# Edge attention on one NeuronCore: TensorE's weighted sums of batch b-2 stand in front of the transposes of batch b instead of behind them

## The reference, cut to what matters

```python
Q = (h @ Wq.T + bq).reshape(-1, H, DH)
K = (h @ Wk.T + bk).reshape(-1, H, DH)
V = (h @ Wv.T + bv).reshape(-1, H, DH)
scores = jnp.einsum('ehd,egd->ehg', Q[src], K[tgt]) / jnp.sqrt(jnp.float32(DH))
attn = jax.nn.softmax(scores, axis=-1)
msg = jnp.einsum('ehg,egd->ehd', attn, V[tgt]).reshape(-1, HID)
msg = msg + Ee[et]
proj = msg @ Wo.T + bo
return jax.ops.segment_sum(proj, src, num_segments=n_nodes)
```

## Time and profile before

| What | us |
|---|---|
| median of 3 runs | 7294.34 (7294.27 to 7296.85) |
| the profiled execution's own time | 7286.34 |
| its span, first to last instruction | 7284.5 |
| VectorE busy in the span | 5184.5 (71%) |
| GpSimd busy | 4463.2 (61%) |
| TensorE busy, products | 4321.9 (59%) |
| mean granted clock of TensorE | 0.823 of full speed |

### The profile page before, as it was taken

The page is one execution under the profiler, slowest core; times in us unless marked ns, Lnnn a source line. Parts: engine busy times, 40 slices in busy tenths (PEclk is TensorE's granted clock), DMA queues, the critical chain, the costliest instruction groups (busy, mean ns, idle before and its releaser), DMA issues. The chain is left out here.

```text
span 7284.5 us, 179506 instructions
## 1 busy us (share of the span) xinstructions
PE 4321.9 (59%) x60555; PEld 3475.4 (48%) x60555; DVE 5184.5 (71%) x12108; ACT 1183.6 (16%) x2828; POOL 4463.2 (61%) x3974
## 2 busy tenths in 40 slices
PE   0000388885245546788877788876888885355541
PEld 0000266663134435677765677764777764133331
DVE  6999877777445565677765677755777755688877
ACT  0000022220011111122210222210222211122210
POOL 5888777777177730777751777741777740577720
PEclk9999999995555558999998999998999997555555
DMA  0000000001144433666613666614676510344420
GB/s 30 1 4 1 2 1 1 1 1 27 30 123 131 131 85 110 182 201 193 185 34 118 188 198 192 175 31 125 191 201 193 165 27 10 98 111 111 110 63 18
DMA packets 708570, 691.60 MB, mean 95 GB/s; under 512 B 234981, under 2 KB 589355, under 8 KB 708165
## 3 DMA queue, kind: packets, MB, share of 16 engines
q0 software_dynamic: 227328, 446.06, 22.5%
q1 hardware_dynamic: 480846, 240.51, 11.9%
HBM read 766.03 MB, written 77.58 MB: 116 GB/s over the span
## 5 line engine op out<-in xcount | busy, mean ns | idle before, releaser
L1669 POOL DMA_INDIRECT kvring<-kvtab,oth x1776 | 1973.5, 1111 | 822.5 <-issue 420.4
L1069 POOL DMA_INDIRECT e_hg<-htab,oth_d x992 | 1014.9, 1023 | 817.4 <-issue 763.5
L1720 PE MATMUL ea_pss<-ea_qb,ea_kT 128*128 128x128 f32 x7104 | 1020.5, 277 | 0.0
L1720 PEld LDWEIGHTS ea_pss<-ea_qb,ea_kT 128*128 128x128 f32 x7104 | 946.3, 194 | 16.3
L1764 ACT ACTIVATE ea_kT<-ea_pst 128x512 f32<-128x512 f32 x888 | 482.0, 594 | 2013.4 <-PE ea_pst L1708 1984.2
L1708 PE MATMUL ea_pst<-ident,kvring 128*128 128x128 f32 x3552 | 488.2, 281 | 464.7 <-DMA kvring<-kvtab,oth 464.3
L241 POOL DMA_INDIRECT steps<-or_rec,or_rplacei x392 | 567.5, 1448 | 135.0 <-issue 135.0
L1708 PEld LDWEIGHTS ea_pst<-ident,kvring 128*128 128x128 f32 x3552 | 385.5, 142 | 543.0 <-DMA kvring<-kvtab,oth 332.3
L1804 DVE TENSOR_REDUCE ea_sc<-ea_pss 128x64 f32<-128x1024 f32 x444 | 540.8, 1218 | 53.1 <-PE ea_pss L1720 53.0
L1832 DVE TENSOR_TENSOR ea_mix<-ea_hot,ea_att 128x1024 f32<-128x1024 f32 (+1 forms) x444 | 544.9, 1227 | 0.2
L1731 PE MATMUL ea_psg<-ea_mix,kvring 128*64 128x64 f32 x14208 | 518.1, 227 | 12.8 <-DVE ea_mix L1832 12.8
(11 more groups left out here) (506 smaller groups left out, 8332.7 us busy)
## 6 DMA issues: line engine op xcount, KB each, us to landing
ea_qb<-qtab SPq DMA_DIRECT2D x1776, 64.0 KB
qtab<-at_qst SPq DMA_DIRECT2D x75, 512.0 KB, 3.3
kvring<-kvtab,oth POOLq DMA_INDIRECT x1776
e_stack<-ohtab SPq DMA_DIRECT2D x744, 32.0 KB
kvtab<-at_kvst SPq DMA_DIRECT2D x75, 256.0 KB, 2.7
e_hg<-htab,oth_d POOLq DMA_INDIRECT x992
ea_mk<-mtab SPq DMA_DIRECT2D x444, 3.0 KB
htab<-Hd SPq DMA_DIRECT2D x2, 3200.0 KB, 11.6
```

The lines of the kernel that those rows point to most:

```text
L1069: pool.indirect_dma_start(out=hg[:, b % RING, u, :], out_offset=None, in_=htab, in_offset=bass.IndirectOffsetOnAxis(ap=oth[:, b * 4 + u:b ...
L1669: pool.indirect_dma_start(out=kv[:, b % R, u, :], out_offset=None, in_=kvtab, in_offset=bass.IndirectOffsetOnAxis(ap=oth[:, b * QB + u:b * ...
L1720: mm = pe.matmul(ps_s[r % 2][:, u, k * 2 * HN:(k + 1) * 2 * HN], kT[:, r % 2, u, k, :], qb[:, r, u, :], start=False, stop=True, skip_group ...
```

## The change

In the two places of TensorE's list where `turn` and `gather` are called together, the call of `gather(b - 2)` moves in front of `turn(b)`. Nothing is added or removed, and the lists of the other four engines are the same, row for row.

```diff
                 for r in range(1, R):
-                    turn(r, 0, r, True)
                     if r >= 2:
                         gather(r - 2, 0, r - 2, False)
+                    turn(r, 0, r, True)
                     score(r, 0, r, r >= 2)
                 with pe.Fori(1, NQ // R) as i:
                     for r in range(R):
                         b = i * R + r
-                        turn(b, i, r, True)
                         if r >= 2:
                             gather(b - 2, i, r - 2, True)
                         else:
                             gather(b - 2, i - 1, r + 2, True)
+                        turn(b, i, r, True)
                         score(b, i, r, True)
```

## The result

The changed kernel takes 7564.57 us (median of 4 runs, 7561.62 to 7567.53), the kernel before 7295.6 us in the same comparison (7294.27 to 7303.79, 4 runs). The ratio is 1.036, with a 95% interval of 1.034 to 1.038. The profiled execution took 7562.66 us, with a span of 7560.9, against 7286.34 before.

The account below looks back on a forecast made before the run. GpSimd's gather pace was taken as the bound, 5.60 us a batch; a new closed loop of 6.22 us adds 266.5 us, layer starts 12 and the profile-to-median gap 8, giving 7573 us, range 7470 to 7640.

Parts of the forecast that it names:

- The bound of before: GpSimd's gather issues, one per 1.41 us and four a batch, set the old period of about 5.6 us.
- The closed loop: Transposes, spread, exponential, weights, sums, then transposes again: 6.22 us a batch, +266.5 us over 432 periods.
- The last term: On TensorE, from the first sum to the first transpose: 1.12 us, kept between 1.00 and 1.25.
- the leg: From the start of the transposes to the end of the weights, over ScalarE and VectorE: 5.00 us.
- Nothing gained behind the transposes: On TensorE, the sums were hidden behind ScalarE's spread, so scores still start 2.27 us after the transposes.
- The starts of the layers: Batches 2 and 3 of each layer now wait for the weights: 4.0 us a layer, 12 us in all.
- The wait for rows: TensorE's 464.3 us wait for gathered rows ahead of the transposes goes, with 4.7 us to spare.
- The rival by which it falls: TensorE's clock falls to 1.2 GHz: 9.4 us a batch, about 8950 us; chance 3%.
- The 8 us: Added to the kernel's summed time because the profiled execution before was 8.0 us below the median of the runs.
- it simply issues as fast as it can: GpSimd's gathers are not held back by the ring's free slots, as gaps between issues are always 0.30 us.
- 250 us of waits for `ea_psg`: Sign of being right: GpSimd's L1669 waits for TensorE's sums, about 0.6 us a batch.
- The rival "faster": Sums signalled earlier free GpSimd from the ring: 5.2 us a batch, -173 us, 7121 us; chance 3%.

Follow-up runs that it names:

- Experiments 5 and 7: 5: changed kernel with VectorE's L1832 done twice per batch, 8133.49 us. 7: changed kernel with VectorE's four takes ahead of its wait for the exponential, 7406.72 us.
- experiment 3: Changed kernel without the gathers after the first four batches of a layer, later batches reusing those rows: 7569.0 us, 1.037 of before.
- experiment 8: Changed kernel with ScalarE's list turned round, the exponential of batch b-1 ahead of the spread of batch b: 7380.26 us, 1.010 of before.
- experiment 2: Changed kernel with L1832's weights `att` kept in PSUM instead of SBUF: 7565.86 us, 1.037 of before.

## Why the prediction was right, point by point

The forecast was 7573 us, the time is 7564.57.

- **The bound of before** was taken to be GpSimd's issues. Right: with the gathers gone the order of before falls by 435 us or 1.0 us a batch, and with GpSimd freed of the stretches by 182 us or 0.42 us a batch, to 5.20 in the mean.
- **The closed loop**, the main term: 5.00 + 0.10 + 1.12 = 6.22 us were forecast, 4.98 + 0.14 + 1.09 = 6.21 were measured. The three misses, -0.02, +0.04 and -0.03, cancel; that they come to 0.01 together is luck. The last term had no row in the trace before and came out between its two neighbours, 1.04 and 1.13. The range's +164 and +367 us were reckoned from 5.60 us; from the 2420.5 us of the sum they are 163 and 366, which changes nothing. Experiments 5 and 7 lengthened and shortened the leg, and the time followed by 1.28 and -0.36 us a batch (the mean periods by 1.28 and -0.37); experiment 3 took away the gathers and changed nothing; experiment 8 cut the loop between the spread and the exponential, and the wait for the weights went.
- **Nothing gained behind the transposes.** Right: the scores start 2.26 us after them (3199.88 and 3202.14), 2.27 before, and TensorE stands idle there for 1.18 us.
- **The starts of the layers**, forecast at 4.0 us each. Batch 3 follows 5.75 us after batch 2, not 6.2, so that it is about 3.5 us.
- **The wait for rows** was to vanish but for the first batch of each layer, 73.6 us remain. Waits of about 200 us for `ea_mix` and 500 us for `ea_kT` were forecast; they are 206 and 532.
- **The clock** stayed at 1.00, 2.4 GHz, over the 900 us of each layer looked at, with TensorE busy for 74% of the time. The rival by which it falls did not come. The transposes ran at the full clock, 1.09 us for eight; whether they count as busy is something no run here can tell.
- **The 8 us** between the profiled execution and the median are most of the miss of 8.4 us: the profiled execution after lies 2 us below its median, not 8. The other 2 us are the loop (262 us and not 266.5) and the starts (10 and not 12), less some 4 us from outside both, of which 3 came ahead of the first layer. So the sum is better than its parts.

**One step was wrong, without harm to the number.** It was "it simply issues as fast as it can", argued from gaps of 0.30 us beside every issue. A part of the issues was not at its own pace: VectorE's L1832 held up those that fell into it, which the mean of 1.11 us against the usual 1.00 could have told. From the same step came the forecast that L1669 would show 250 us of waits for `ea_psg`. They are 135.7 us, the ordinary gap in 432 batches, and the spare time went into stretched issues. That it did no harm is shown by experiment 2, in which the stretches are gone and the time is the same. It was not foreseen, and the reason is in the rows: a held issue ends 0.87 us after L1832, and behind it follow a gap and three issues of 1.30 us, so that the next fourth issue starts 0.87 + 0.30 + 3 x 1.30 = 5.07 us after L1832's end. The next L1832 starts 6.21 - 1.23 = 4.98 us after it. So the issue falls into L1832 again, 0.1 us behind its start, as in the batch above (3203.74 and 3203.63), and GpSimd takes on the loop's period without waiting for the ring. The forecast's sentence that the wait for the rows hides inside the new period held: experiment 3 has no rows to wait for and the same time. The rival "faster" priced GpSimd's free pace at 5.2 us a batch and 173 us less; that pace is real, 7114 us, but what opens it is L1832's operand and not the order of the sums.

## What to carry to other kernels

Before a group is moved ahead of another on an in-order engine, follow its input back: if it comes from the last result of the group that it now precedes, by way of other engines, the move closes a loop. If that loop is longer than every other bound, the period is the loop's length, whatever each engine's share. A wait that one moves work into is only free if the work's own input is there when the wait begins; here it came 0.32 us later, and the work was longer than what was left. A two-operand VectorE instruction on SBUF beside gathers issued by GpSimd is worth one look: moving its small operand to PSUM took 2.5% off this kernel, the fastest version here that does all of the work, and it keeps the order of before.

## What the runs showed of the hardware that was not expected

An indirect DMA's issue on GpSimd that starts while VectorE multiplies two SBUF operands (1.23 us) ends 0.87 us after that instruction, so that it lasts up to 2.05 us instead of 1.00. One that starts first is not delayed (at most 1.05 us in 373 cases of before), and neither is the VectorE instruction that begins inside it (1.23 us in the mean). The profile counts the delay as GpSimd's busy time: its busy total rose from 4463.2 to 4719.7 us in the changed kernel, with the same instructions. With one operand in PSUM the delay is gone and the VectorE instruction takes the same time, 1.22 us.
